# An attention with fp32 probabilities, written anew with fp16 halves of them held stationary in TensorE

## The reference, cut to what matters

```python
xn = layernorm(x, ln_x_g, ln_x_b)             # context, 256 rows per batch
ln = layernorm(latents, ln_l_g, ln_l_b)       # 256 rows per batch
q = (ln @ Wq).reshape(b, m, h, d)             # 16 heads of 64
kv = concatenate([xn @ Wkv, ln @ Wkv], axis=1)   # 512 keys
qn = rmsnorm(q, qn_g) * scale; kn = rmsnorm(k, kn_g)
sim = einsum('bhid,bhjd->bhij', qn, kn)       # 256 x 512 per head
attn = softmax(where(mask, sim, max_neg))
out = einsum('bhij,bhjd->bhid', attn, v)
return out @ Wout + bout
```

## Time and profile before

| what | us |
|---|---|
| median of 3 runs (1442.98 to 1446.23) | 1444.24 |
| the profiled execution, its own time | 1436.58 |
| its span, first to last instruction | 1434.8 |
| PE, DVE, ACT, POOL busy | 1091.6, 1061.0, 789.7, 442.0 |
| TensorE's granted clock, mean | 0.893 of 2.4 GHz |

### The profile page before, as it was taken

How to read it: one execution, slowest core, us unless ns; L and a number is a source line. 1 busy time by engine, 2 the same in 40 slices (tenths; PEclk the granted TensorE clock), 3 DMA queues, 4 the chain that set the end, 5 groups by cost and what they waited for, 6 DMA issues and landing times. The chain is left out here.

```text
span 1434.8 us, 23644 instructions
## 1 busy us (share of the span) xinstructions
PE 1091.6 (76%) x7405; PEld 710.0 (49%) x7410; DVE 1061.0 (74%) x1847; ACT 789.7 (55%) x1340; POOL 442.0 (31%) x410
## 2 busy tenths in 40 slices
PE   1378888437999414899989899898989989936737
PEld 0245555313444202466666566565656666733426
DVE  8478888675666687777888788888778888646941
ACT  2246666623545324677777677776777676632112
POOL 7001010024777305322333321333312333001135
PEclk9789999767999755899999999999999999967969
DMA  4302010000000200000000000000000000050040
GB/s 183 90 4 25 13 24 0 25 12 12 22 22 16 92 0 1 1 1 1 1 1 0 0 0 0 0 0 0 0 0 0 0 0 1 1 201 1 14 134 27
DMA packets 22587, 33.22 MB, mean 23 GB/s; under 512 B 3856, under 2 KB 19711, under 8 KB 21446
## 3 DMA queue, kind: packets, MB, share of 16 engines
q1 hardware_dynamic: 21096, 29.74, 7.1%
q0 software_dynamic: 1440, 2.82, 0.6%
HBM read 26.52 MB, written 8.77 MB: 25 GB/s over the span
## 5 line engine op out<-in xcount | busy, mean ns | idle before, releaser
L1430 PE MATMUL e_mix<-e_probs,e_v_ones 128*128 128x256 f32 x1024 | 280.9, 394 | 3.8 <-ACT e_mixed L1499 2.4
L1291 POOL TENSOR_TENSOR e_raw<-e_raw,e_inv 128x512 f32<-128x512 f32 x96 | 115.0, 1205 | 384.8 <-DVE e_inv L1557 384.8
L1430 PEld LDWEIGHTS e_mix<-e_probs,e_v_ones 128*128 128x128 f32 x1024 | 179.9, 194 | 45.5 <-issue 25.2
L1574 DVE TENSOR_REDUCE e_row_max<-e_row_scores 128x1 f32<-128x512 f32 x256 | 165.6, 680 | 16.3 <-PE e_row_scores L1359 15.9
L1522 ACT ACTIVATE e_probs<-e_scores 128x512 f32<-128x512 f32 x256 | 142.2, 599 | 26.3 <-PE e_scores L1418 25.1
L1299 POOL TENSOR_TENSOR e_natural<-e_raw,e_natural 128x512 f16<-128x512 f32 x96 | 114.7, 1194 | 60.1 <-DVE e_natural L1568 60.1
L1359 PE MATMUL e_row_scores<-e_k_high,e_q_high 65*128 65x512 f16 x256 | 90.6, 388 | 55.0 <-DVE e_row_max L1574 50.0
L1418 PE MATMUL e_scores<-e_q_high,e_k_high 128*128 128x256 f16 x512 | 129.2, 285 | 0.0
L1417 PE MATMUL e_scores<-e_q_stack,e_k_stack 128*128 128x256 f16 x512 | 128.6, 285 | 0.0
L1614 DVE RECIPROCAL e_inverse<-e_summed 128x256 f32<-128x256 f32 x64 | 111.7, 1746 | 7.4 <-ACT e_mixed L1499 7.2
L1542 DVE TENSOR_REDUCE e_sum_sq<-e_squares 128x8 f32<-128x512 f32 x96 | 65.7, 685 | 62.3 <-ACT e_squares L1470 61.0
(11 more groups left out here) (361 smaller groups left out, 2597.6 us busy)
## 6 DMA issues: line engine op xcount, KB each, us to landing
w<-in_w SPq DMA_DIRECT2D x2, 2048.0 KB, 10.0
c_w<-in_w SPq DMA_DIRECT2D x17, 192.0 KB, 2.4
placed_scratch<-in_no_rows SPq DMA_DIRECT2D x1, 2313.0 KB, 16.2
a_mask_q<-in_mask_q SPq DMA_DIRECT2D x1, 2048.0 KB, 10.3
a_mask_k<-in_mask_k SPq DMA_DIRECT2D x1, 2048.0 KB, 14.7
parts_scratch<-a_parts SPq DMA_DIRECT2D x2, 1024.0 KB, 4.0
k_stack<-parts_scratch SPq DMA_DIRECT2D x24, 64.0 KB
q_stack<-parts_scratch SPq DMA_DIRECT2D x24, 64.0 KB
```

Source lines behind the costliest of these rows:

```text
L1291: nc.gpsimd.tensor_tensor(raw[:, j], raw[:, j], bc(inv[:, HU * j:HU * j + HU], (P, HU, D1), 2), ALU.mult).then_inc(normed, 1)
L1430: mm = pe.matmul(mix[:, 0:S], v_ones[par][:, kt, h, :], probs[buf][:, kt, :], start=(kt == 0), stop=(kt == KT - 1))
L1574: dve.tensor_reduce(row_max[:, i, qt:qt + 1], row_scores[qt][:], AX.X, ALU.max).then_inc(max_done, 1)
```

## The change

The probabilities are computed twice, in fp32 and fp16; VectorE subtracts for the low half of the even head (`lo` 0), GpSimd for the odd head (`lo` 1). Both halves are stationary, 128 keys by 128 queries, and 65 columns of fp16 values move (64 and a one for the sum), with a second 64 for the values' low half. The result has queries down, so sums are one column; VectorE divides it from PSUM, TensorE turns it (`a`), ScalarE copies it for the output projection. Values have two halves; VectorE writes the low one and so empties the bank. Row scores have one bank, exact scores two of 4 tiles each. `raw` is double: q and k are projected, and the root taken, one unit earlier, two ahead of their use. The high rows and the maxima are placed by transfers from SP, and the maxima come negated from the reduction, are turned in fp32, and pass through `neg_rows`. The turned halves are copied as fp32 words.

```diff
-JOBS = [[("q", t) for t in range(QT)] + [("v", t) for t in range(3)],
-        [("v", t) for t in range(3, KT)] + [("tk", t) for t in range(2)],
-        [("tk", t) for t in range(2, KT)] + [("tq", t) for t in range(QT)],
-        [("k", t) for t in range(KT)]]
-SPLITS = [[("root",)], [("split", j) for j in range(4)], [("split", j) for j in range(4, 6)], []]
-ROOT_AT = 12
+KQ = [("k", t) for t in range(KT)] + [("q", t) for t in range(QT)]
+VALUES = [[0, 1, 2], [3], [], []]
+TURNS = [[], [("tk", 0), ("tk", 1)], [("tk", 2), ("tk", 3), ("tq", 0), ("tq", 1)], []]
+RAWS = [KQ[0:1], KQ[1:2], KQ[2:3], KQ[3:6]]
+SPLITS = [[0, 1], [2, 3], [4, 5], []]
 NEWTON = 3
 RSQRT_BITS = float(0x5f3759df)
-M_AT = 2
+VC1 = 2 * D1 + 2
 def plan_step(s, first, last):
...
+    hf, p = divmod(s, PU)
+    produce, project = not (last and hf), not last
+    ahead, behind = not (last and s == 2 * PU - 1), not (first and s == 0)
+    norms = [[("norm", j), ("hi", j), ("low", j)] for j in SPLITS[p]] if produce else []
+    early = [("o",)] if s == 2 and not first else []
+    early += [("a",)] if not (first and s < 2) else []
+    raws = RAWS[p] if project else []
+    values = [("v", t) for t in VALUES[p]] if produce else []
+    turns = TURNS[p] if produce else []
+    jobs = early + (turns[:2] + raws + values + turns[2:])
+    w = [[("w", i)] if behind else [] for i in range(2)]
+    r = [[("r", i, qt)] if ahead else [] for i in range(2) for qt in range(QT)]
+    m = [("m",)] if ahead else []
+    n0, n1 = (norms[i] if norms else [] for i in range(2))
+    lo1, n = ([("lo", 1)], [("n",)]) if behind else ([], [])
+    jobs = jobs + [None] * 8
+    def job(k):
+        return [jobs[k]] if jobs[k] else []
+    if p < PU - 1:
+        out = n0[:1] + r[0] + w[0] + lo1 + job(0) + r[1] + n0[1:2] + job(1) + [("s", 0)] + n0[2:] + r[2] + n1[:1] \
+            + w[1] + job(2) + r[3] + n + n1[1:2] + job(3) + m + n1[2:] + job(4) + [("s", 1)] + [("lo", 0)] + job(5) + job(6) + job(7)
     else:
...
+        out = w[0] + lo1 + job(0) + [("s", 0)] + r[0] + job(1) + w[1] + r[1] + job(2) + r[2] + n + job(3) + r[3] + job(4) + m \
+            + [("s", 1)] + [("lo", 0)] + job(5) + job(6) + job(7) + ([("root",)] if project else [])
...
+FIRST_UNIT = KQ + [("root",)]
+for _j in range(6):
+    FIRST_UNIT += [("norm", _j)] + ([("v", _j)] if _j < KT else []) + [("hi", _j), ("low", _j)]
+FIRST_UNIT += [("tk", t) for t in range(KT)] + [("tq", t) for t in range(QT)]
+NEXT_UNIT = KQ + [("root",)]
+FIRST_ROWS = [("r", i, qt) for i in range(2) for qt in range(QT)] + [("m",)]
+START = FIRST_UNIT + FIRST_ROWS + NEXT_UNIT
+END = [("lo", 1), ("w", 0), ("w", 1), ("n",), ("a",), ("a",), ("o",)]
...
-        v_ones = [sb(f"v_ones{i}", [P, KT, HU, P], F32) for i in range(2)]
-        raw = sb("raw", [P, 6, HU, D1], F32)
+        v_cols = [sb(f"v_cols{i}", [P, KT, HU, VC1], F16) for i in range(2)]
+        raw = [sb(f"raw{i}", [P, 6, HU, D1], F32) for i in range(2)]
-        row_max = sb("row_max", [P, 2, QT], F32)
-        neg_max = sb("neg_max", [P, 2 * QT, P], F16)
-        mixed = [sb(f"mixed{i}", [P, S], F32) for i in range(2)]
-        summed = [sb(f"summed{i}", [P, S], F32) for i in range(2)]
-        inverse = sb("inverse", [P, S], F32)
-        attended = sb("attended", [P, H1 // 2, S], F32)
-        row_scores = [psum(f"row_scores{i}", [P, NK1]) for i in range(QT)]
-        scores = [psum(f"scores{i}", [P, 2, S]) for i in range(3)]
-        mix = psum("mix", [P, 512])
+        p_hi = [sb(f"p_hi{i}", [P, KT, S], F16) for i in range(2)]
+        p_lo = [sb(f"p_lo{i}", [P, KT, S], F16) for i in range(2)]
+        neg_max = [sb(f"neg_max{i}", [P, 2 * QT], F32) for i in range(2)]
+        neg_rows = [sb(f"neg_rows{i}", [2 * QT, P], F16) for i in range(2)]
+        inverse = sb("inverse", [P, 2, QT], F32)
+        attended = [sb(f"attended{i}", [P, QT, P], F32) for i in range(2)]
+        attended_t = sb("attended_t", [P, H1 // 2, S], F32)
+        row_scores = psum("row_scores", [P, NK1])
+        scores = [psum(f"scores{i}", [P, KT, S]) for i in range(2)]
+        mix = psum("mix", [P, 2, S])
+        mixed = mix[:, :, 0:QT * (D1 + 1)].rearrange("p i (t c) -> p i t c", t=QT)
...
+            def copy_high(event, use, par):
+                sp.wait_ge(misc_taken[use[0]], use[1] + 1)
+                name, t = event
+                cols = slice(P * t, P * t + P)
+                if name == "tk":
+                    dma = sp.dma_start(k_high[par][0:D1, :, cols], k_stack[par][0:D1, :, cols])
+                else:
+                    dma = sp.dma_start(q_high[par][0:D1, :, cols], q_stack[par][D1:P, :, cols])
+                dma.then_inc(high_in, 16)
+            def place_max(use, par, p):
+                sp.wait_ge(misc_taken[use[0]], use[1] + 1)
+                row = q_high[par][MROW1:MROW1 + 1, 2 * p:2 * p + 2, :].rearrange("o h (t c) -> o (h t) c", c=P)
+                sp.dma_start(row, neg_rows[p % 2][:]).then_inc(max_in, 16)
...
+            def low_probs(q, i):
+                pool.wait_ge(exp_done, 2 * (2 * q + i + 1))
+                nc.gpsimd.tensor_tensor(p_lo[i][:], probs[i][:], p_hi[i][:], ALU.subtract).then_inc(lo_done[i], 1)
...
-                    mm = pe.matmul(bank[:, P * i:P * i + P], neg_max[:, i, :], ident16[:], start=True, stop=True)
+                pe.wait_ge(max_done, 4 * (q + 1))
+                pe.transpose(bank[0:2 * QT, 0:P], neg_max[buf][:], ident32[:]).then_inc(ready, 1)
+            def rows(q, par, p, i, qt):
+                n = 4 * q + 2 * i + qt
+                if not (isinstance(n, int) and n == 0):
+                    pe.wait_ge(max_done, n)
+                h = 2 * p + i
+                pe.matmul(row_scores[:], q_high[par][0:MASK1 + 1, h, P * qt:P * qt + P], k_high[par][0:MASK1 + 1, h, :],
+                          start=True, stop=True).then_inc(rows_ready, 1)
+            def weigh(q, i, par, p):
+                pe.wait_ge(lo_done[i], q + 1)
+                if not (isinstance(q, int) and q == 0):
+                    pe.wait_ge(att_done, q)
+                h = 2 * p + i
+                for qt in range(QT):
+                    at = slice(P * qt, P * qt + P)
+                    out = mix[:, i, (D1 + 1) * qt:(D1 + 1) * (qt + 1)]
+                    for kt in range(KT):
+                        values = v_cols[par][:, kt, h, :]
+                        first, last = qt == 0 and kt == 0, kt == KT - 1
+                        pe.matmul(out, p_hi[i][:, kt, at], values[:, 0:D1 + 1], start=first, stop=False, skip_group_check=True)
+                        pe.matmul(out[:, 0:D1], p_hi[i][:, kt, at], values[:, D1 + 1:2 * D1 + 1], start=False, stop=False, skip_group_check=True)
+                        mm = pe.matmul(out, p_lo[i][:, kt, at], values[:, 0:D1 + 1], start=False, stop=last, skip_group_check=True)
+                mm.then_inc(weighed, 1)
+            def turn_attended(use, q, buf):
+                bank, ready = emptied(use)
+                pe.wait_ge(att_done, q + 1)
+                for qt in range(QT):
+                    mm = pe.transpose(bank[:, P * qt:P * qt + P], attended[buf][:, qt, :], ident32[:])
...
                         elif name == "s":
-                            i, half = rest
+                            i = rest[0]
                             h = 2 * p + i
...
+                            if i == 0:
+                                pe.wait_ge(max_in, 16 * (q + 1))
+                            if not (bt.first and s == 0):
+                                pe.wait_ge(exp_done, 2 * (2 * q + i - 1))
+                            for kt in range(KT):
+                                out = scores[i][:, kt, :]
+                                cols = slice(P * kt, P * kt + P)
+                                pe.matmul(out, k_stack[hf][:, h, cols], q_stack[hf][:, h, :], start=(kt % 2 == 0), stop=False, skip_group_check=True)
+                                mm = pe.matmul(out, k_high[hf][:, h, cols], q_high[hf][:, h, :], start=False, stop=True, skip_group_check=True)
                             mm.then_inc(scored, 1)
...
+            def take_raw(event, use, u, par):
...
+                act.copy(raw[par][:, j], heads(bank))
+                if not (isinstance(u, int) and u == 0 and j < 2):
+                    act.wait_ge(summed_sq, 6 * u + j - 1)
+                act.activation(squares[j % 2][:], heads(bank), ACT.Square).then_inc(taken, 1)
+            def take_values(event, use, u, par):
+                bank, _ = filled(use)
+                if not (isinstance(u, int) and u < 2):
+                    act.wait_ge(weighed, HU * (u - 1))
+                act.copy(v_cols[par][:, event[1], :, 0:D1], heads(bank)).then_inc(v_high, 1)
+            def take_turned(event, use, par):
+                name, t = event
+                bank, taken = filled(use)
+                stack = k_stack[par] if name == "tk" else q_stack[par]
```

(37 more changed lines are left out.)

475 lines of the change are left out of this document (200 added, 275 removed).

## The result

| | before | after |
|---|---|---|
| median, us (runs of the same chip) | 1443.61 (1441.71 to 1446.23) | 1549.93 (1544.84 to 1556.93) |
| ratio | | 1.0738, 95% interval 1.0692 to 1.0785 |
| profiled execution; span | 1436.58; 1434.8 | 1548.52; 1546.7 |
| granted clock of TensorE, whole kernel | 0.893 | 0.861 |

The kernel is slower by 106 us, the profiled execution by 112.

The account below looks back on a forecast made before the run. VectorE's in-order queue was taken as the bound: 32.0 us work plus 16.4 waits, 48.4 per unit against 43.6. Seven batches add 67, start 11, tail 2: +80, forecast 1524 us, range 1400 to 1580, its own case 1480 to 1550.

Parts of the forecast that it names:

- VectorE's own work: VectorE's operations per unit (half the heads of one batch) in the second attention: 32.0 us against 35.8 before.
- The steps of a unit: Four steps of two heads, VectorE's work plus waits: 12.5, 9.9, 10.1 and 15.95 us, 48.4 per unit against 43.6.
- One sign: Among the things that would show the forecast: VectorE's casts should average above 0.8 us.
- The sum: Whole second attention: seven batches at 2 x 4.8 = 9.6 us more, 67; with start and tail, +80 us.
- Start, last batch and tail: Ends of the second attention: 11 us more at the start; shrinking last-batch waits but a tail, 2 us.
- The transfer: 128 KB of high rows moved by SP before the fourth step's row matmul: taken as 3.0 us, bounds 2.4 to 3.7.
- rival (d): Transfers block one another on SP's queue, maxima placed behind copies: 1 to 2 us more per unit; chance 0.13 with (c).
- GpSimd and SBUF: Low probabilities, both inputs in SBUF, might wait for GpSimd: up to 1 us per unit, 16 us in all.
- rival (c): TensorE's granted clock falls to 0.83 from 0.98: 2.4 us more per unit, 1563 us; chance 0.13 with (d).
- TensorE's values at nothing: Values as 24 fp16 matmuls per head, about 0.027 us apart: gain of 1.6 us per unit, beside VectorE's queue, counted at nothing.
- The bound is VectorE's queue: Second attention before the change: VectorE, run in order, 35.8 us busy and 7.8 us of waits per unit.
- The price of one bank: One row-score bank instead of two: the second maximum waits 0.5 us in step 1, 0.75 in steps 2 and 3.

Follow-up runs that it names:

- experiment 8: Changed kernel with GpSimd's low-half subtraction for the odd head cut to 16 of 1024 elements: 1528.0 us, ratio 1.0603 to the kernel before.
- experiment 1: Changed kernel with the output projection moved from the third step of a batch to the fourth, into the wait for the transfer: 1537.0 us.
- kernel 7: Changed kernel with tiles split and turned sooner and the first head's low half placed sooner in VectorE's order, both together: 1517.5 us.
- Edits 2: Changed kernel with the four value projections of a unit spread one to a step, instead of three in the first and one in the second: 1562.1 us.
- 3: Changed kernel with projections, sums, second head's scores and first head's low half put ahead of the fourth step's first row scores: 1567.5 us.
- 5: Changed kernel with tiles split and turned sooner, three in the first step of a unit: 1547.05 us, ratio 1.0759 to the kernel before.
- 6: Changed kernel with the first head's low half earlier in VectorE's order instead of at the step's end: 1539.8 us.
- experiment 10: Kernel before the change, with both row scores of a head through one bank: 1672.0 us, ratio 1.1635.
- kernel 12: Kernel 9 with two row-score banks, each row matmul one place ahead of its maximum, and three score banks of 512 columns: 1495.7 us.
- kernel 4: Changed kernel with the queries' high rows copied by VectorE instead of by transfer, the keys' still by transfer: 1516.05 us.
- kernel 9: Kernel 7 with each sum of squares one maximum later on VectorE and the output projection in two halves: 1509.9 us.

## Why the prediction was right, and where it was off

The side was right, and the time, 1524 forecast and 1549.9 measured, lies in the range of 1400 to 1580 and at the very end of the forecast's own, 1480 to 1550. Part of the closeness is luck: 2.2 us too much work per unit stands against 3.6 us too little waiting, of which the output projection is 2.1. Point by point:

- **VectorE's own work.** 32.0 us per unit forecast; 31.7 measured, in which are the 1.9 us that casts and gains wait for GpSimd (experiment 8: 29.8 without them) and that I had put under waits. So it is 2 us less than forecast, and idle and contended time together (18.1 + 1.9) 1.5 us more than my 16.4 + half of the output projection's 4.2 would give.
- **The steps of a unit.** 12.5, 9.9, 10.1, 15.95 forecast; 12.4, 10.2, 9.4, 16.6 in the unit without the output projection, 48.6 us against 48.4. Right, and the single waits are at their places: the third low value 2.07 (1.65), the first low value 1.03 (0.6), the first cast 1.57 us long behind GpSimd, 1.15 of it waiting (1.5), the first maximum of the fourth step 4.5 us (4 to 5), with the transfer as what TensorE waits for. One sign failed: casts were to average above 0.8 us and averaged 0.71 in the five batches; GpSimd was busy 42.9 us per batch (45).
- **The term that failed.** "The sum" counted the unit twice per batch and gave the output projection nothing. It stands in the third step of a batch ahead of the second row matmul, and VectorE's add is ahead of everything else: 4.2 us per batch, 8 batches. With it 9.6 per batch would have been 13.8; measured 12.4. By experiment 1 only 1.4 of the 4.2 come back when it is moved, so this term's own size is not measured. It is what my own list of events showed, and I costed it nowhere; in the kernel before it hid behind VectorE's backlog.
- **Start, last batch and tail.** 13 us forecast. The last add to the residual moved by 107.6 us (1268.4 to 1376.0), of which 7 batches of 12.4 make 87 and a later start of the stage (its first projection, 542.3 to 544.9) 2.6, so 18. It falls at the start: the first add is 38.3 us later, and the last two intervals between adds together only 6.2 longer. An estimate from these: nearly 20 for the start (11 forecast), and the end a little shorter (2 longer forecast). Behind the last add another 4.3 us are lost (172.5 against 168.2), outside the change.
- **The transfer.** Taken as 3.0 us, bounds 2.4 to 3.7; the trace shows 2.6 from issue to landing, and TensorE's waits for it in the five batches:

```profile
PE e_row_scores L1403 <- DMA e_q_high<-e_q_stack: 19.9, 10, 2.1
e_k_high<-e_k_stack SPq DMA_DIRECT2D x64, 128.0 KB, 2.6
e_q_high<-e_q_stack SPq DMA_DIRECT2D x32, 128.0 KB, 2.6
```

  With the rate that the Trainium skill gives in DMA: Bandwidth & Descriptors, section Where 436 GB/s comes from, the estimate was about 2.0 (1.7 of the earlier trace rows and 0.3); the measurement lies between and decides. It is TensorE's only wait for a transfer there, so rival (d), in which the placing of the maxima comes late, did not come true.
- **GpSimd and SBUF.** By the Trainium skill, SBUF — State Buffer, section Who interferes with whom, the low probabilities, with both inputs in SBUF, would wait for a GpSimd operation that reads SBUF. The trace agrees: of 64 the median is 1.22 us, and one that begins at 1074.58, while GpSimd subtracts from 1074.14 to 1075.29, takes 1.80. But they seldom meet. In four batches 32 of them average 1.289 us, 0.6 us per batch above the median, where the rule at its word gave 2.
- **The clock.** 0.91 in these batches and not 0.83, and not below the 0.9 that I named; but rival (c) was not nothing. What it costs shows inside the changed kernel. The two fourth steps of a batch have the same events. Behind the wait for the transfer one of them has the upper level of the clock (2.4 GHz), the other for nearly all of the stretch the lower (1.2 GHz). Two stretches (PE, PEld, DVE, ACT, POOL, then clock, DMA share, GB/s), and VectorE's wait for the first square in each:

```profile
1034.00:1037.00 3.00, 2.23 (x31) 1.22 (x29) 1.92 (x3) 1.82 (x4) 0.00 (x0) 1.00 0.00 0
1035.78 0.69 DVE L1617 TENSOR_REDUCE e_sum_sq<-e_squares 128x8 f32<-128x512 f32 x1 [1.07 <-ACT e_squares L1533]
1080.36:1083.00 2.64, 2.64 (x24) 1.72 (x25) 0.69 (x1) 1.02 (x3) 0.00 (x0) 0.53 0.00 0
1083.26 0.69 DVE L1617 TENSOR_REDUCE e_sum_sq<-e_squares 128x8 f32<-128x512 f32 x1 [1.71 <-ACT e_squares L1533]
```

  In the second the projection's matmuls are 0.43 us apart and not 0.22, the next square comes later too (1.17 for 0.32), and from the first maximum to the end of the root VectorE needs 11.8 us and not 10.45. Five of the ten units in the window have the longer wait for this square (1.45 to 1.71 us). So at this one place the clock takes some 1.3 us per batch of the 12.4. TensorE had stood still for 1.9 us before the slow stretch and for 2.1 before the other, so the length of the last pause does not decide it.

  Over the window the score matmuls average 301 ns against 284 before (273 is their median in both); taken for all of TensorE's work that is 6%, some 3 us of my 56 per batch, an estimate. And executions of one kernel differ, with the clock in most cases: kernel 8's by 15.6 us for 0.010 (above), kernel 1's by 17.8 for 0.017 (1543.0 at 0.851, 1525.2 at 0.868), kernel 7's by 18.3 for 0.008 (1526.1 at 0.841, 1507.8 at 0.849), the changed kernel's by 12.1 for 0.012 (1556.9 at 0.846, 1544.8 at 0.858), though its 1548.5 stands at 0.861. From 1 to over 2 us per thousandth: at the lower rate the 0.032 between 0.893 and 0.861 could be worth some 30 us of the 106. That is an estimate from pairs of runs, and what is cause in it is open, since between two kernels a lower mean can also be the consequence of longer waits: in the changed kernel's window 1037.00 to 1044.30, where VectorE does its last maxima and the root, it is 0.67, and in 1062.00 to 1074.00 it is 1.00. Over the experiments batch and clock go together only loosely (99.0 us at 0.87, 94.6 at 0.88, 93.5 at 0.92, 92.1 at 0.91). I had it as a rival of small chance, where it is a term that belongs in the sum.
- **TensorE's values at nothing.** Their pace is as forecast: 24 of them with 65 or 64 columns take from 1067.11 to 1067.83, 0.03 us apart. Right to count at nothing, in themselves.
- **"The bound is VectorE's queue."** Half right. The waits I listed are there, but the explanation behind them, that a wait removed is time gained, fell. Edits 2, 3, 5 and 6 took 6 to 30 us out of one kind of wait in five batches and put 15 to 37 into another. The account that fits all runs is this: TensorE, ScalarE and VectorE go through one list of events with little between them, the row scores in one bank tie them 32 times per batch, and the chain from the last turned tile through ScalarE, the transfer and the row matmul ends a unit at about the time that the rest does. The price of one bank, "0.5" and "0.75" per step in my sums, holds for the order that the change brings with it; in the order before, experiment 10, it is 31.6 us per batch. In the changed order the second bank, paid for with a bank of scores, gave back 1.4 (kernel 12).

**What stays open.** The 12.4 us per batch can't be divided fully. Edits 4 and 9 returned 3.7 and 6.1, and were not tried together; two banks returned 1.4 more on top of 9. The rest, 4.9 us with kernel 12 (92.1 against 87.2), may be the exponentials in pairs, the low halves on the way from exponentials to values, or the clock, of which 1.3 us per batch are seen at one place of the changed kernel; none of these was separated by an experiment. Nor was the clock in the edits that won nothing: in the windows of 2, 3 and 5 it is 0.87 to 0.88 and not 0.91. No version here beats the kernel before.

## What to carry to other kernels

Count the places where two queues must meet, not only the work in each: in the kernel before, a second buffer between a producer and a consumer that both run in order was worth 32 us per batch of 87 (given back to the changed order, 1.4), and a copy of 0.4 to 1.3 us on the busiest engine was better than a transfer of 2.6 us that freed it, because it was the last link of the chain. When a long wait is removed, look for the chain that ends just behind it before counting the gain; two edits worth nothing and 0.3% alone gave 1.9% together. A wait can cost more than its length, since TensorE may come out of it at the lower clock. And go through the new list of events for everything that stands in it once per batch: the rarest one was the term I missed.

## What the runs showed of the hardware

Executions of the same program differ by up to 1.2% in time, mostly with their mean granted clock, without any edit (kernel 8: 1521.7 us at 0.869, 1537.3 at 0.859), so a gain below 1% should not be read from one execution of each.

An engine that catches up can meet more contention: with the same operations on GpSimd, casts of VectorE went from 0.73 us on average in the changed kernel to 0.83 in kernel 9 and 1.04 in kernel 12, single ones to 2.33, as more of them start beside GpSimd's subtraction of 2.13 us (the one of 2.33 us begins at 1103.69, the subtraction at 1103.61); without that subtraction they take 0.42. Copies of the high rows of the queries took 0.42 us in the kernel before and 1.27 in kernel 4, single ones that met the subtraction 1.98.

Behind a wait of about 2 us TensorE went on at the lower clock in some units and at the upper in others; at the lower, matmuls of 64 or 65 moving columns are 0.055 us apart and not 0.030, those of 512 columns 0.43 and not 0.22.

A transfer of 128 KB within SBUF, in pieces of 256 bytes, lands after 2.6 us, hardly later than one of 192 KB in large pieces (2.4).
